# Moving the attention of all four sequences into the first stage of a fused decoder layer

## The reference

```python
x = _layernorm(x + attn(x, ...))                 # 16 heads of width 16, decayed scores, no softmax
x = _layernorm(x + xattn(ctx_1024, x, ...))      # a state-space recurrence over the context, 256 channels x 16 states
x = _layernorm(x + ffn(x, ...))                  # gated feed-forward, 896 wide, 2 of 8 low-rank experts
```

```python
dmask = jnp.where(diff >= 0, gamma[:, None, None] ** expn, 0.0)
scores = jnp.einsum('bhnd,bhmd->bhnm', q, k) * dmask
ret = jnp.einsum('bhnm,bhmv->bhnv', scores, v)
norm = (ret - mean) * jax.lax.rsqrt(var + EPS)   # mean and var over each head's positions and widths
gate = jax.nn.silu(x @ wg + bg)
out = gate * ro @ wo + bo
```

## Time and profile before

| what | us |
|---|---|
| median of 3 runs | 450.38 |
| lowest and highest run | 449.34, 452.68 |
| span of the profiled execution (first to last instruction) | 447.4 |

### The profile page before, as it was taken

The page is one execution under the profiler, slowest core; times in us unless marked ns, Lnnn a source line. Parts: engine busy times, 40 slices in busy tenths (PEclk is TensorE's granted clock), DMA queues, the critical chain, the costliest instruction groups (busy, mean ns, idle before and its releaser), DMA issues. The chain is left out here.

```text
span 447.4 us, 7104 instructions
## 1 busy us (share of the span) xinstructions
PE 390.1 (87%) x2552; PEld 331.3 (74%) x2552; DVE 321.1 (72%) x622; ACT 184.3 (41%) x416; POOL 226.8 (51%) x219
## 2 busy tenths in 40 slices
PE   3869776798899999987999999987999998989993
PEld 2547554567689898665789888665899897789982
DVE  4384859647988996876788996877988996732234
ACT  2695593448423522567123522567224332221110
POOL 6065579005766993043556993034585982051131
PEclk9996957689999999998699999999999999999998
DMA  7998200002111130030121130030112100000000
GB/s 236 110 359 320 116 0 23 0 23 98 33 64 49 61 108 8 5 94 23 48 72 50 57 101 21 3 96 23 72 48 96 69 3 0 1 25 0 1 1 23
DMA packets 14962, 28.45 MB, mean 64 GB/s; under 512 B 1864, under 2 KB 5712, under 8 KB 14672
## 3 DMA queue, kind: packets, MB, share of 16 engines
q1 hardware_dynamic: 14016, 24.18, 18.0%
q10 hardware_dynamic: 912, 3.83, 2.2%
HBM read 26.56 MB, written 1.44 MB: 63 GB/s over the span
## 5 line engine op out<-in xcount | busy, mean ns | idle before, releaser
L942 PE MATMUL xf<-am,wsplit 128*128 128x256 f32 x672 | 91.7, 286 | 1.9 <-DVE work L1753 1.4
L942 PEld LDWEIGHTS xf<-am,wsplit 128*128 128x128 f32 x672 | 83.4, 189 | 6.2 <-issue 3.5
L507 POOL TENSOR_TENSOR ring<-cv,brow 128x512 f32<-128x512 f32 x48 | 75.8, 1593 | 15.0 <-PE acc L942 14.8
L909 ACT ACTIVATE fth<-xf 128x256 f32<-128x256 f32 x56 | 21.4, 382 | 137.8 <-PE xf L942 137.8
L614 POOL TENSOR_TENSOR work<-work,ratioT 128x256 f32<-128x256 f32 x28 | 26.9, 962 | 67.0 <-DVE work L1753 64.6
L942 PE MATMUL a2p<-work,wff_sb 128*128 128x256 f32 x224 | 57.9, 380 | 1.8 <-POOL work L614 1.8
L1742 DVE SCALAR_TENSOR_TENSOR fth<-fth,xf 128x256 f32<-128x256 f32 x56 | 23.2, 414 | 43.8 <-ACT fth L909 43.5
L942 PE MATMUL xf<-x2s,wsplit 128*128 128x256 f32 x336 | 48.7, 294 | 0.5 <-ACT work L883 0.5
L942 PE MATMUL acc<-ident,ring 128*128 128x128 f32 x256 | 41.2, 293 | 7.5 <-POOL ring L544 6.4
L942 PEld LDWEIGHTS xf<-x2s,wsplit 128*128 128x128 f32 x336 | 43.2, 193 | 3.3 <-issue 2.2
L942 PEld LDWEIGHTS acc<-ident,ring 128*128 128x128 f32 x256 | 32.8, 151 | 14.8 <-POOL ring L544 7.7
(11 more groups left out here) (214 smaller groups left out, 702.0 us busy)
## 6 DMA issues: line engine op xcount, KB each, us to landing
brow<-bc_dram SPq DMA_DIRECT2D x24, 256.0 KB, 3.4
crow<-bc_dram SPq DMA_DIRECT2D x24, 256.0 KB, 3.2
work<-in_wsp SPq DMA_DIRECT2D x2, 896.0 KB, 7.2
wff_sb<-in_wff SPq DMA_DIRECT2D x2, 896.0 KB, 7.1
am<-bc_dram ACTq DMA_DIRECT2D x1, 1536.0 KB, 9.5
wattn_sb<-in_wattn SPq DMA_DIRECT2D x1, 1280.0 KB, 5.6
xT_sb<-in_xT SPq DMA_DIRECT2D x4, 256.0 KB, 3.7
xn_sb<-in_x SPq DMA_DIRECT2D x4, 256.0 KB, 2.6
```

The lines of the kernel that those rows point to most:

```text
L507: pool.tensor_tensor(ring[:, i % RING], du[:, j].unsqueeze(1).broadcast_to([P, UN, S]), brow[:, c % 2], ALU.mult).then_inc(sem["drive_read ...
L909: act.activation(fth[:, n % 2], xf[XF_BANK[X_MAIN + n]][:, 0], ACT.Tanh, scale=0.5).then_inc(sem["th_ready"], 1)
L942: return pe.matmul(o, l, r, skip_group_check=True, **kw)
```

## The change

- **Where attention is done.** Stage 0 now does attention and first norm of all four sequences. `turn(i)` maps unit i of the recurrence to sequence s = (i + 2) // 4 and a quarter r = (i + 2) % 4; each unit does one scores call and the r-th part of the rest: r = 0 keys, GATE, second values call of the sequence before; r = 1 V, mean, output of the one before that; r = 2 first values call, variance, next Q; r = 3 state, next K. Two scores calls of sequence 0 and Q of sequence 1 come before unit 0. The last parts of sequences 2 and 3 follow the loop, and output, residual and norm of sequence 3 come behind the seam. Normed rows of all sequences are kept in `x1` (4 sequences wide). Stages 1 to 3 only read them (`z_input`, `z_gate`).
- **Banks.** `gen` becomes a rotation of three PSUM banks (the third is `a2p0`), `values` alternates between `a2p1` and `ret`, drives use two banks instead of three, and the transposed `du` is copied to SBUF. So drive(i) waits for scan i - 1 where it waited for i - 2.
- **Masks.** The power row, its trip through DRAM and the mask transfers go. VectorE makes each head's mask by a scan over the identity matrix, 16 scans, and 2 for `qdec`, each of 128 columns.
- **Values.** Two calls of 32 instructions on four column groups instead of four calls of 16 on two; `sc` has four buffers instead of two.
- **W2 sums.** `DOWNS` starts at piece 5 instead of 9, in every stage; in the last stage sums 5 and 6 are left for the end. `base` of piece 1 is always done ahead of the loop.
- **Prelude order.** K is projected before the low-rank step; on ScalarE keys and mask copies come before the logarithm; SP loads the first of the split weights at once; the DRAM trip of B and C moves from ScalarE's queue to SP's.

```diff
-DOWNS = {9: (0,), 10: (1, 2), 11: (3,), 12: (4,)}
-DOWNS_LAST = {9: (0,), 10: (1,), 11: (2,)}
+DOWNS = {5: (0,), 6: (1,), 9: (2,), 10: (3,), 12: (4,)}
...
+def turn(i):
+
+    return (i + 2) // 4, (i + 2) % 4
...
+        gens = [gen[0][:], gen[1][:], a2p[0][:].rearrange("p t s -> p (t s)")]
+        rets = [a2p[1], ret]
+        drives = [xf[0], xf[1]]
+        duT = xpad[:, :, DC - 1:]
...
             def drive(b, i):
 
                 j, c = i % 2, i // 2
-                if i == 2:
-                    pe.wait_ge(sem["bT_ready"], 1)
-                need(pe, "state_ready", b, max(i - 2, 0))
+                need(pe, "state_ready", b, max(i - 1, 0))
...
+            def values(s, t):
+
+                o = rets[s % 2]
+                need(pe, "sc_ready", s, 4 * t + 4)
...
                 for chunk in range(2):
                     cs = slice(chunk * P, (chunk + 1) * P)
                     for p_ in range(2):
-                        for k in range(2):
...
+                        for w in range(4):
+                            last = mm(o[32 * w:32 * w + 32, t, cs],
...
                 for i in range(UNITS):
+                    s, r = turn(i)
+                    if s < B:
+                        scores(s, r)
+                    if r == 2 and s < B:
+                        values(s, 0)
+                    if r == 0:
+                        values(s - 1, 1)
+                    if i + 2 < UNITS:
                         drive(b, i + 2)
...
+                    if r == 0:
+                        if s < B:
+                            token_keys(s)
+                        project(s - 1, "GATE", wg)
+                    if r == 1:
+                        if s < B:
+                            token_values(s)
+                        group_mean(s - 1)
+                        if s > 1:
+                            attention_out(s - 2)
+                    if r == 2 and s > 0:
+                        group_var(s - 1)
+                        if s + 1 < B:
+                            project(s + 1, "Q", wq)
+                    if r == 3:
+                        chunk_state(s)
+                        if s + 1 < B:
+                            project(s + 1, "K", wk)
                     if i == 14:
                         token_z(b)
+                    if i > 0:
+                        add_states(b, i - 1)
+                group_var(B - 1)
                 context(nb)
                 add_states(b, UNITS - 1)
-                need(pe, "x_in", nb, 16)
-                project(nb, "Q", wq)
                 seam(b, None, None)
                 low_rank(nb)
+                attention_out(B - 1)
...
+            def masks(h0, h1):
+
+                for h in range(h0, h1):
+                    dve.tensor_tensor_scan(dmask[:, h], gamma_sb[:, h:h + 1].broadcast_to([P, P]), ident[:], 0.0,
+                                           ALU.mult, ALU.add).then_inc(sem["mask_step"], 1)
...
             def first(b, nb):
 
+                dve.wait_ge(sem["w_gamma"], 16)
+                dve.wait_ge(sem["pool_const"], 4)
+                masks(0, 8)
                 conv(b)
...
+                for i in range(4):
+                    decayed(0, i)
                 for i in range(UNITS):
+                    s, r = turn(i)
+                    if r == 0 and s > 2:
+                        norm_shift(s - 3, mv1, rs1, nm1, "r1_pow", "r1_shift")
+                    if r == 1:
+                        group_stats(s - 1)
+                    if r == 3 and s > 0:
+                        group_scale(s - 1)
                     first_scan(b, i)
+                    if s < B:
+                        decayed(s, 2 * r)
+                        decayed(s, 2 * r + 1)
+                    if r == 0 and s < B:
+                        token_keys(s)
+                    if r == 1:
+                        if s < B:
+                            token_values(s)
+                        group_mean(s - 1)
+                    if r == 2 and s > 1:
+                        attended(s - 2)
+                    if r == 2 and s > 0:
+                        group_var(s - 1)
+                        gate_silu(s - 1)
+                    if r == 3:
+                        chunk_state(s)
                     if i == 0:
-                        chunk_state(b)
...
+                gate_silu(B - 1)
+                group_var(B - 1)
+                attended(B - 2)
+                group_scale(B - 1)
+                norm_shift(B - 2, mv1, rs1, nm1, "r1_pow", "r1_shift")
...
                 seam(b, nb)
+                attended(B - 1)
+                norm_shift(B - 1, mv1, rs1, nm1, "r1_pow", "r1_shift")
...
                 spread_rows(fb, X_MD)
-                if b is not None:
-                    project(b, "K", wk)
-                    token_values(b)
-                    token_keys(b)
-                else:
-                    base(fb, 1)
+                base(fb, 1)
                 spread_rows(fb, X_RW)
-                if b is not None:
-                    project(b, "GATE", wg)
-                    chunk_state(b)
-                    scores(b, 0)
```

More of the change, by code:

```diff
@@ L24 @@
 RING = 4
[L25 to L27 removed]
+CONSTS = 19 + E
 VEC = {}
@@ L1314, in seam @@
                     context(nb)
[L1315 to L1316 removed]
                 if fb is not None:
[L1318 removed]
+                    for m in range(sum(len(ms) for ms in DOWNS.values()), FM - (nb is not None)):
                         down(fb, m)
@@ L1402, in stage @@
                 else:
-                    down(fb, FM - 1)
+                    for m in range(sum(len(ms) for ms in DOWNS.values()), FM):
+                        down(fb, m)
                     end_sum(fb)
@@ L1733, in stage @@
                         scan(b, units[0])
-                    if b is not None and n < 4:
-                        decayed(b, 2 * n)
-                        decayed(b, 2 * n + 1)
-                    last = n == 11
-                    if units and not last:
                         times_c(b, units[0])
```

874 lines of the change are left out of this document (412 added, 462 removed).

## The result

| what | before | changed |
|---|---|---|
| median | 450.97 | 471.59 |
| lowest and highest of 4 runs | 449.34, 452.68 | 470.53, 472.39 |
| span of the profiled execution | 447.4 | 469.4 |

The changed kernel is slower: ratio 1.050, 95% interval 1.043 to 1.057. The forecast was 450.0, with a range of 437 to 464. First the page of the changed kernel (span, busy time of each engine, granted clock in 40 slices), to be read against the earlier trace rows.

What follows compares the result with a forecast made beforehand. TensorE, 87% busy, with VectorE at 72%, leaves nothing idle enough for free work. Stages 138.5+83+77.5+77.5+69.6 = 446.1; median 3.0 above the span, 449.1; +1 for a low clock: 450, range 437 to 464.

Steps and rivals of the forecast that it cites:

- Prelude: Start of first stage up to scan 0: mask scans of 0.36 each, 6.5 in all; scan 0 near 35.5, 6.5 later.
- I laid a turn of four units out in queue order: First-stage loop of 16 units: a turn takes 24.7, set by VectorE's chain with waits of 6.1; TensorE 21.8.
- 18.3 and 8x0.44: TensorE's work in a turn: attention 18.3, fewer values calls, drive and sum 8x0.44, given as 21.8.
- Rival (c): First-stage units in lockstep across TensorE and VectorE: 7.0 a unit instead of 6.2, total 461; decides from 6.6; chance 0.18.
- over 148: First flip of x2, ending the first stage: forecast 138.5; over 148 would mean rival (c) or (d).
- 1.00 from 45 to 120: First-stage loop: TensorE's granted clock would be 1.00 from 45 to 120 us.
- Rival (d): New first-stage loop at a clock of 0.75 too: +17 or so, total 467; chance 0.10.
- Heads: Starts of stages 1 to 3: first hidden piece 18.5 after the flip in stages 2 and 3; stage 1's chain 21.8.
- the 85 that the forecast had named: Later stages: one keeping over 85 us would mean VectorE's chain or GpSimd's drives bound it.
- VectorE: 57.4 less 14 is 43 of 51, no bound: Stage 3's loop: without attention's 14, VectorE is busy 43 of 51 and does not bound; loop and tail 59.
- The 77.5: Stages 2 and 3 without attention: 77.5 each, from head 18.5 and loop and tail 59.
- The low end of 1.2: Values call of 32 instructions on four column groups: 1.2 if all overlap, up to 2.4; 1.5 taken.

Runs made afterwards that it cites:

- when moved: Changed kernel with VectorE's scale of the group norm behind the scan and score products instead of ahead of the scan: 468.39, first flip 3.9 sooner.
- reordered kernel: Changed kernel with projections ahead of the drive, values ahead of scores, Q of sequence 1 in unit 0, norm scale behind scan and products: 462.06, flip 139.6.
- narrow drives: Changed kernel with GpSimd's 16 drive products of stages 1 to 3 covering 32 of 256 columns, the rest left out: 461.59.
- the second drive later: Reordered kernel with GpSimd's drive of unit 1 moved behind its sum of the masks: 465.77.
- the base moved: Kernel before with only the base of piece 1 put ahead of the loop: 446.11 against 453.0 run beside it, ratio 0.987.
- the same edit in both kernels: GpSimd's drive products cut to 32 of 256 columns in stages 1 to 3: kernel before 442.87 against 449.89, changed kernel 461.59.

## Why the prediction was wrong

- **Prelude: right.** Scan 0 at 35.7 for 35.5. A mask scan takes 0.38 from start to start for 0.36.
- **The 16 units: the step "I laid a turn of four units out in queue order", with waits of 6.1 a turn, failed.** VectorE's waits, 6.1 a turn in the sum, measured 7.6, 10.7 and 7.6 (turn less busy time), while its work, 18.6 a turn in the sum, was 15.5, 17.6 and 17.4; so an excess of work hid part of the waits that were missing. Units 0 and 1 took 13.9 for 10.0. The first flip came 9.8 late. Two links were missing. First, VectorE's products of a new pair wait for values, which stand behind K's projection, which stands behind a drive that waits for the scan (4.8 and 4.0 at two starts of a sequence; 3.6 in unit 0 behind Q of sequence 1). Second, the scale of the norm was costed as work, not as a wait ahead of a scan (3.9 when moved). TensorE's work was 20.7, 25.6 and 20.0 for 21.8, near it in the mean only; and 18.3 and 8x0.44 are 21.8 already, so the sum did not take off the two values calls that it names. The reordered kernel comes within 1.1 of the forecast flip, with errors of either sign in its parts, which is in part luck. Rival (c), lockstep, is the nearest in kind, but it was to decide from 6.6 a unit and the units took 6.4 in the mean, in steps from 3.2 to 9.1: the waits lie at certain units, not in each. The sign "over 148" for the flip came true at 148.25.
- **The clock, "1.00 from 45 to 120": wrong,** 0.97, 0.94 and 0.87 in the three turns and 0.75 in units 0 and 1. Rival (d), 0.75 throughout, did not come, though every unit has its transposes (of the two it names, the drives are; the sums are ordinary matmuls with the identity). No run here shows whether they count for the clock, since the waits lie in the same stretches.
- **Heads: 18.5 forecast, 19.6 measured.** Expert products ended when forecast (low halves begin 17.8 after the flip), but two low halves took 2.3, not 1.3, because GpSimd's drives now fall on them (1.3 again with the second drive later). In stage 1 the head took 23.3 for 21.8 (TensorE's first hidden piece at 171.53), at a clock of 0.72; the sum had 2.2 for this clock. Stage 1 keeps 86.3, over the 85 that the forecast had named as its sign of being wrong, and for the reason it gave, VectorE beside GpSimd's drives, at least in part: 83.1 with narrow drives.
- **Loop and tail: "VectorE: 57.4 less 14 is 43 of 51, no bound" failed.** It was busy 49.5 of 55.7: only 7.9 went from the loop. Of the 14, some 2 to 3 lay in the head and not in the loop, and 3.4 came back as longer products and scans (the products 12.5 to 15.0, the scans 12.1 to 13.0). The sum took TensorE's lost work as time saved one for one; TensorE lost 16.1 of busy time in stage 3 and the stage 12.4, as its idle time grew from 7.3 to 11.0.
- **Stage 2's baseline: the clock booked as attention's.** Its 101.0 is 6.3 longer than stage 3; with the base moved it is 95.8, and only 1.6 longer. The granted clock in the 101.0 is 0.50 to 0.81 from 202.5 to 207.5 and from 212.5 to 220, and 1.00 in all of stage 3. The 77.5 does not rest on it, since the sum puts stage 3's loop behind stage 2's head; but some 5 of the 23.5 booked as saved in stage 2 was never attention's.
- **What is left.** With narrow drives the three stages take 239.4, and the forecast was 238. So all but 1.4 of the 13.6 missed goes with the drives' width, which stands for the hold-up and GpSimd's longer queue together. Part of that was there before the change: with the same edit in both kernels the saving is 46.4 (285.8 to 239.4), without it 40.0, and 53.6 was forecast. What the change itself uncovered is the 3 to 6.5 from above. How the rest splits between clock and waits was not separated.
- **Values: mis-sized.** A call takes 1.1, under the 1.5 taken. The low end of 1.2 was a mean over both clocks; at the full clock a call of before takes 1.07 and one of the changed kernel 1.08. The Trainium skill (TensorE: Matmul & The Clock Gate, section "Packing small matmuls — row/col tiling") has matmuls on different column groups run at the same time, which gives the low end, and the trace agrees. In the kernel before, what it saves on TensorE did not shorten the time (0.996, an interval that holds 1).
- **Last stage and W2 sums: right,** 69.5 for 69.6. Median less span was 2.2 for 3.0.

The range missed because the cases were kept apart: rival (c) priced a poor order in the new stage, and no case priced a poor return in the old ones, let alone both. Together they make the 23.3.

## What to carry to other kernels

Work moved into an idle stage pays only if the order of each queue lets it: ask of every instruction that waits what stands behind it and needs not wait, and put that first. Here that was needed and not enough: the reordered kernel is still slower (1.026). Work taken off the busiest engine is worth less than its duration where a second engine is nearly as full, and its going uncovers what lay beside it. Look first for a gap that existing work can fill without new waits: one moved call gave 1.3% here, where the large move cost 5%.

## What the runs showed of the hardware that I had not expected

- A scan of 512 columns on VectorE takes 1.19 to 1.23 with one operand in PSUM, beside full and narrow drives alike, and 1.2 up to 2.2 with both in SBUF beside GpSimd's products; a product with C takes 0.69 to 1.75. GpSimd's products are lengthened too: with narrow drives in both, a drive of an eighth of the columns takes 0.32 in the median in the kernel before and 0.76 in the changed kernel, 0.31 at the least in either.
- Sixteen more instructions on two more column groups cost nothing visible: 1.07 for 16, 1.08 for 32.
- The same wait of 2.3 on TensorE, in the same place of the program, was followed by the lower clock in four of six stages (a projection of 3.4 to 3.7) and not in the other two (2.0). What decides it no run here shows. A wait of 0.9 was followed by 2.0 in all four.
